# Transposes of 128x128 blocks on TensorE split into pairs of 64-row halves, with every engine's order rebuilt

## The reference, cut to what matters

```
scores = jnp.einsum('bach,baCh->bacC', k, q)
attn = jax.nn.softmax(masked / np.float32(np.sqrt(D_HEAD)), axis=-1)
z = jnp.einsum('bacC,baCh->bach', attn, v)
...
q = l2norm(q) * qs
k = l2norm(k) * ksc
q, k = rotary_xpos(q, k)
o = local_attention(q, k, v)
x = x + o @ wo
...
h = a * jax.nn.gelu(g, approximate=False)
x = x + h @ w2 + b2
```

## Time and profile before

| | |
|---|---|
| median of 3 runs | 1154.78 us (1153.16 to 1154.82) |
| the profiled execution's own time | 1154.38 us |
| its span, first to last instruction | 1152.6 us |
| PE busy | 1124.3 us, 98% of the span |
| PEld busy | 874.4 us, 76% |
| DVE, ACT, POOL busy | 790.9, 691.6 and 610.0 us |
| PE clock | granted 0.996 of full speed over the span |

### The profile page before, as it was taken

How to read it: one execution, slowest core, us unless ns; L and a number is a source line. 1 busy time by engine, 2 the same in 40 slices (tenths; PEclk the granted TensorE clock), 3 DMA queues, 4 the chain that set the end, 5 groups by cost and what they waited for, 6 DMA issues and landing times.

```text
span 1152.6 us, 20639 instructions
## 1 busy us (share of the span) xinstructions
PE 1124.3 (98%) x7114; PEld 874.4 (76%) x7114; DVE 790.9 (69%) x2417; ACT 691.6 (60%) x1712; POOL 610.0 (53%) x641
## 2 busy tenths in 40 slices
PE   8999999999999999999999999999999999999997
PEld 6777777777777766767667887877878878787676
DVE  6867677667767356778897677768667686675553
ACT  3668677777767224453676647657656566575832
POOL 1456666666664322049896446557465474573330
PEclk9999999999999999999999999999999999999999
DMA  7003333323210401030040001200002100001010
GB/s 255 1 2 132 100 109 113 123 93 123 89 71 2 164 19 55 1 112 22 19 176 1 2 1 36 94 1 1 1 19 99 55 1 1 1 32 42 19 38 18
DMA packets 30310, 64.72 MB, mean 56 GB/s; under 512 B 3840, under 2 KB 16256, under 8 KB 29696
## 3 DMA queue, kind: packets, MB, share of 16 engines
q1 hardware_dynamic: 30208, 63.41, 15.7%
HBM read 41.04 MB, written 22.36 MB: 55 GB/s over the span
## 4 chain that ended last, share of the span: by engine, by line
PE 90%; DVE 4%; POOL 2%; ACT 2%; issue 1%; DMA 0%; DVEq 0%; ACTq 0%; POOLq 0%
PE psum L1532 48%; PE psum L1633 7%; PE psum L1598 6%; PE psum L1615 6%; PE psum L1765 5%; PE psum L1814 5%; PE psum L1799 4%; PE psum L1781 4%; PE psum L1747 2%; PE psum L1827 1%; PE psum L1838 1%; PE psum L1721 1%; POOL rn L780 1%; PE psum L1829 0%; DVE y L1091 0%
## 5 line engine op out<-in xcount | busy, mean ns | idle before, releaser
L735 POOL TENSOR_TENSOR probs<-probs,rden 128x128 f32<-128x128 f32 (+3 forms) x256 | 177.6, 725 | 80.6 <-DVE rden L1149 80.6
L974 ACT ACTIVATE lp<-lp,lneg,rn 128x256 f32<-128x256 f32 (+1 forms) x256 | 143.6, 568 | 11.6 <-DVE lneg L1366 11.5
L890 ACT ACTIVATE probs<-probs,negmax 128x128 f32<-128x128 f32 (+3 forms) x256 | 139.9, 553 | 5.8 <-DVE negmax L1144 5.8
L1134 DVE CUSTOM_DVE_ANT_0 probs<-psum,causal 128x128 f32<-128x128 f32 (+3 forms) x256 | 110.3, 487 | 19.4 <-PE psum L1598 19.3
L768 POOL TENSOR_TENSOR lp<-lp,lrden 128x128 f32<-128x128 f32 x64 | 25.6, 400 | 165.8 <-DVE lrden L1371 165.8
L780 POOL TENSOR_TENSOR rn<-ssm,neg_half 128x8 f32<-128x8 f32 x64 | 108.4, 1693 | 0.0
L1354 DVE CUSTOM_DVE_ANT_0 lp<-psum,local 128x256 f32<-128x256 f32 (+1 forms) x256 | 84.2, 385 | 20.6 <-PE psum L1765 20.6
L771 POOL TENSOR_TENSOR lp<-lp,lrden 128x768 f32<-128x768 f32 x64 | 93.9, 1467 | 0.0
L1532 PE MATMUL psum<-wqkv_hi,hT_lo 128*128 128x512 f32 x192 | 82.0, 427 | 0.1
L961 ACT ACTIVATE sq<-psum 128x512 f32<-128x512 f32 x64 | 38.0, 594 | 68.9 <-PE psum L1532 68.9
L1633 PE MATMUL psum<-pT,v 128*64 128x256 f32 (+3 forms) x512 | 77.7, 446 | 1.4 <-DVE pT L1158 1.0
(11 more groups left out here) (172 smaller groups left out, 3146.7 us busy)
## 6 DMA issues: line engine op xcount, KB each, us to landing
w_raw<-in_w_all SPq DMA_DIRECT2D x22, 380.0 KB, 3.1
w_scratch<-w_half SPq DMA_DIRECT2D x22, 380.0 KB, 2.3
w_scratch<-w_rest SPq DMA_DIRECT2D x22, 380.0 KB, 3.0
x<-in_x SPq DMA_DIRECT2D x8, 512.0 KB, 7.4
aw<-in_w_quads SPq DMA_DIRECT2D x4, 768.0 KB, 5.5
wqkv_lo<-w_scratch SPq DMA_DIRECT2D x6, 512.0 KB, 6.3
wqkv_hi<-w_scratch SPq DMA_DIRECT2D x6, 512.0 KB, 4.5
w_hi<-w_scratch SPq DMA_DIRECT2D x2, 1364.0 KB, 6.5
```

Source lines behind the costliest of these rows:

```text
L735: ins = pool.tensor_tensor(pr, pr, rden[:, u % 2, h, i:i + 1].broadcast_to([P, TRI[i]]), ALU.mult)
L890: ins = act.activation(pr, pr, ACT.Exp, bias=negmax[:, u % 2, h, i:i + 1], scale=ADH ** -0.5, accum_out=den[:, u % 2, h, i:i + 1])
L974: ins = act.activation(pr, pr, ACT.Exp, bias=lneg[:, u % 2, h, w:w + 1], scale=rn[:, m % 2, w, 0, 2 * j + h:2 * j + h + 1], accum_out=lden ...
L1134: ins = dve.tensor_tensor_reduce(probs[:, u % 2, h, TRI_AT[i]:TRI_AT[i + 1]], bank[:, at:at + TRI[i]], causal[:, S - TRI[i]:S], 1.0, -3e38 ...
```

## The change

Each transpose of a 128x128 block becomes two: rows 0 to 63 of the block are transposed by the upper half of the array into 64 columns of one bank, rows 64 to 127 by the lower half into 64 columns of another. This is done for all probabilities (causal and local) and for the rotated q and k; transposes of `x`, `y` and the normalized inputs stay whole. The number of copies out of PSUM and their elements stay the same, but their destination has runs of 64 with gaps of 64. The banks, the groups (8, 8 and 4 blocks in a causal unit, two banks each) and all order strings are new.

```diff
-T_BANKS = (4, 5, 2, 3, 4, 5)
-Z_BANK = 4
+T_BANKS = ((4, 5), (2, 3), (4, 5))
...
-T_TILES = ((0,), (1, 3), (2,))
+T_BLOCKS = (((0, 0), (0, 1), (0, 3)), ((1, 0), (1, 1), (1, 3)), ((0, 2), (1, 2)))
...
-        UNIT_PE = ("sA@2 z sB@2 pv@2 pk@3 pq@3 t0@1 t1@1 t2@1 t3@1 t4@1 t5@1")
+        UNIT_PE = ("sB@2 z pk@3 pq@3 pv@3 t0@1 t1@1 sA@3 t2@1")
...
-        UNIT_ACT = ("e0@1 e1@1 pv@2 aw2@2 pk@3 aw0@3 pq@3 aw1@3 t1@1 t3@1 part@1 t5@1")
+        UNIT_ACT = ("e1@-1 pk@1 aw0@1 pq@1 e0 t1@-1 t3@-1 aw1@1 t5@-1 pv@1 part@-1 aw2@1")
...
             if what == "z":
-                take((what, *at), Z_BANK)
+                turn((what, *at), "p")
...
+                if u >= 2 and part == "sA":
+                    for n in (4, 5):
+                        wait_full(dve, plan["t", u - 2, n])
...
-                for c in T_TILES[k]:
-                    for i in range(c, T):
-                        lo = TRI_AT[i] + c * P
-                        ins = pe.transpose(bank[:, at:at + P], probs[:, u % 2, h, lo:lo + P], ident[:, :])
-                        at += P
-                ins.then_inc(full[use[0]], 1)
+            def transposes(u, g):
+
+                pe.wait_ge(s_prob, 2 * u + (1 if g == 0 else 2))
+                uses = [plan["t", u, 2 * g + half] for half in range(2)]
+                banks_of = [wait_free(pe, use) for use in uses]
+                blocks = [(h, i, c) for h, c in T_BLOCKS[g] for i in range(c, T)]
+                for n, (h, i, c) in enumerate(blocks):
+                    lo = TRI_AT[i] + c * P
+                    for half in range(2):
+                        rows = slice(half * HP, (half + 1) * HP)
+                        ins = pe.transpose(banks_of[half][:, n * HP:(n + 1) * HP], probs[rows, u % 2, h, lo:lo + P],
+                                           ident[rows, rows])
+                        if n == len(blocks) - 1:
+                            ins.then_inc(full[uses[half][0]], 1)
...
+                        for half in range(2):
+                            rows = slice(half * HP, (half + 1) * HP)
+                            ins = pe.transpose(banks_of[half][:, at:at + HP], ra[rows, t % 2, i, j * P:(j + 1) * P],
+                                               ident[rows, rows])
...
+                        for half in range(2):
+                            rows = slice(half * HP, (half + 1) * HP)
+                            ins = pe.transpose(banks_of[half][:, at:at + HP], lp[rows, u % 2, h, lo:lo + P],
+                                               ident[rows, rows])
```

More of the change, by code:

```diff
@@ L15 @@
 P = 128
+HP = P // 2
 B, S, D = 4, 512, 256
@@ L312, in unit_at @@
             return c, j, j // 2, 2 * c + j % 2
[L316 to L321, removed]
@@ L388, in build @@
-        CLOSE_POOL = ("sum.0 soft.30.1 soft.31.0 soft.31.1 last.6 norm.7 last.7 sum.1")
+        START_PE = ("xT.0 pq.0 pk.0 xT.1 pv.0 sA.0 sB.0 pk.1 pq.1 pv.1 sA.1 sB.1 pq.2 xT.2 pk.2 t.0.0 pv.2 "
+                    "t.0.1 t.0.2 sA.2 sB.2 z.0 pk.3 xT.3 pq.3")
+        START_DVE = ("xs.0 xn.0 aw.0.0 xs.1 xT.0 aw.0.1 xs.2 xn.1 pq.0 aw.0.2 pk.0 xT.1 xs.3 sA.0 sB.0 pk.1 "
+                     "pq.1 xn.2 sA.1 r.0.0 sB.1 r.0.1 xT.2 pq.2 xn.3 t.0.0 pk.2 t.0.2 t.0.4 sA.2 r.1.0 sB.2 "
+                     "r.1.1 z.0 pk.3 xT.3 pq.3")
@@ L389, in build @@
+        CLOSE_POOL = ("soft.30.1 soft.31.0 soft.31.1 sum.0 sum.1 last.6 norm.7 last.7")
         MLP = ("stats", "sh", "norm", "apply", "hnT", "hT")
@@ L484, in build @@
             if what == "t":
-                take((what, *at), T_BANKS[at[1]])
+                for half in range(2):
+                    take((what, at[0], 2 * at[1] + half), T_BANKS[at[1]][half])
             if what == "z":
-                take((what, *at), Z_BANK)
+                turn((what, *at), "p")
             if what == "awo":
@@ L524, in build, with transposed @@
                 take(("S", at[0], 1, what), 1)
+        def transposed(bank, n):
+            g, half = divmod(n, 2)
+            if g < 2:
+                dst = pT[:, g, 0:KEYB_AT[2]].rearrange("p (b s q) -> p b s q", s=2, q=HP)[:, :, half, :]
+                return bank[:, :].rearrange("p (b q) -> p b q", q=HP), dst
+            dst = pT[:, :, KEYB_AT[2]:TRI_AT[T]].rearrange("p h (b s q) -> p h b s q", s=2, q=HP)[:, :, :, half, :]
+            return bank[:, 0:2 * LOC // 2].rearrange("p (h b q) -> p h b q", h=2, q=HP), dst
         def wait_free(pe, use):
@@ L894, in evac_pT @@
             def evac_pT(u, n):
-                h, k = divmod(n, 3)
                 use = plan["t", u, n]
-                bank = wait_full(act, use)
-                at = KEYB_AT[T_TILES[k][0]]
-                w = sum(KEYB[j] for j in T_TILES[k])
-                copy(pT[:, h, at:at + w], bank[:, 0:w]).then_inc(read[use[0]], 1)
+                src, dst = transposed(wait_full(act, use), n)
+                copy(dst, src).then_inc(read[use[0]], 1)
             def evac_x1T(b):
@@ L981, in evac_T @@
                 bank = wait_full(act, use)
-                copy(lpT[:, h, 0:S], bank[:, :]).then_inc(read[use[0]], 1)
+                copy(lpT[:, h, :].rearrange("p (b s q) -> p b s q", s=2, q=HP)[:, :, 0, :],
+                     bank[:, 0:LOC_N // 2].rearrange("p (b q) -> p b q", q=HP)).then_inc(read[use[0]], 1)
             def evac_O(u):
@@ L1151, in evac_pT @@
             def evac_pT(u, n):
-                h, k = divmod(n, 3)
                 use = plan["t", u, n]
-                bank = wait_full(dve, use)
-                at = KEYB_AT[T_TILES[k][0]]
-                w = sum(KEYB[j] for j in T_TILES[k])
-                dve.tensor_copy(pT[:, h, at:at + w], bank[:, 0:w]).then_inc(read[use[0]], 1)
+                src, dst = transposed(wait_full(dve, use), n)
+                dve.tensor_copy(dst, src).then_inc(read[use[0]], 1)
             def evac_z(u):
@@ L1741, in transposed_qk @@
             def transposed_qk(m, t):
-                for i, (what, done) in enumerate((("Tq", l_q), ("Tk", l_k))):
+                uses = [plan[what, m, t] for what in ("Tq", "Tk")]
+                banks_of = [wait_free(pe, use) for use in uses]
+                for i, done in enumerate((l_q, l_k)):
                     pe.wait_ge(done, T * m + t + 1)
-                    use = plan[what, m, t]
-                    bank = wait_free(pe, use)
                     for j in range(FPAIRS):
-                        ins = pe.transpose(bank[:, j * P:(j + 1) * P], ra[:, t % 2, i, j * P:(j + 1) * P], ident[:, :])
-                    ins.then_inc(full[use[0]], 1)
+                        at = (i * FPAIRS + j) * HP
+                        for half in range(2):
+                            rows = slice(half * HP, (half + 1) * HP)
+                            ins = pe.transpose(banks_of[half][:, at:at + HP], ra[rows, t % 2, i, j * P:(j + 1) * P],
+                                               ident[rows, rows])
+                            if i and j == FPAIRS - 1:
+                                ins.then_inc(full[uses[half][0]], 1)
             def local_scores(u, part):
@@ L1773, in local_transposes @@
                 pe.wait_ge(l_prob, 2 * u + h + 1)
-                for k in range(2):
-                    use = plan["T", u, h, k]
-                    bank = wait_free(pe, use)
-                    at = 0
-                    for c in (2 * k, 2 * k + 1):
-                        for w in range(c, min(c + 2, T)):
-                            lo = loc_at(w) + (P if w == c and w else 0)
-                            ins = pe.transpose(bank[:, at:at + P], lp[:, u % 2, h, lo:lo + P], ident[:, :])
-                            at += P
-                    ins.then_inc(full[use[0]], 1)
+                uses = [plan["T", u, h, half] for half in range(2)]
+                banks_of = [wait_free(pe, use) for use in uses]
+                at = 0
+                for c in range(T):
+                    for w in range(c, min(c + 2, T)):
+                        lo = loc_at(w) + (P if w == c and w else 0)
+                        for half in range(2):
+                            rows = slice(half * HP, (half + 1) * HP)
+                            ins = pe.transpose(banks_of[half][:, at:at + HP], lp[rows, u % 2, h, lo:lo + P],
+                                               ident[rows, rows])
+                            if at == (LOC_N // P - 1) * HP:
+                                ins.then_inc(full[uses[half][0]], 1)
+                        at += HP
             def local_values(u):
```

85 lines of the change are left out of this document (40 added, 45 removed), and 70 rows, old and new, of tables (CLOSE_DVE, ENTRY_ACT, ENTRY_DVE, ENTRY_PE).

## The result

The changed kernel takes 1140.45 us (median of 4 runs, 1139.71 to 1140.73); the kernel before took 1153.97 beside it (4 runs, 1151.73 to 1154.82). The ratio is 0.9885, with an interval of 0.9868 to 0.9902. So the change makes it faster, by 13.5 us and not by the 41 that I forecast. The time lies inside my wide range (1088 to 1153), which was drawn around the rivals too, and outside the 1100 to 1122 that I gave to the forecast by itself.

The account below looks back on a forecast made before the run. PE's instruction list was taken to bound the kernel: 1154.4 - 63.9 (PE alone) + 17.4 (causal loop) + 4.7 (entry and close) + 1 (steps) = 1113.6 us, or 1113; range 1088 to 1153.

Parts of the forecast that it names:

- A pair for 0.06: All 1344 split transposes: a pair of 64-row transposes costs 0.06 us for a block's 0.109, 65.9 us less.
- middle: Rival: a pair costs 0.085 us because of the pace at which four instructions are issued; 1129 us, chance 0.14.
- no-gain: Rival: a pair costs as a block, 0.105 to 0.109 us, loads at the scores' pace; 1151 to 1157, chance 0.09.
- slower: Rival: halves go one after another or at the rows' issue pace, 0.12 us a pair; 1171 us, chance 0.15.
- Modes, 0.2 each: PE's changes of mode go from 282 to 292 at 0.2 us each, 2.0 us more.
- The loop in the causal units, 10.62: A loop through ACT's exponentials and copies, longer than PE's own work, sets the unit at 10.62 us; 17.4 us not had.
- falls inside the same 0.6: Causal units: z's copy and DVE's kl, whose bank pv waits for, add nothing beyond PE's 0.4 to 0.6 us wait.
- PE's own 10.05: Causal unit: PE's own work falls from 11.23 by 20 x 0.049 + 0.2 to 10.05 us.
- I estimate 1 us for all steps: Steps: needing both banks and both copies at once costs 1 us in all; a step saves 3.3 of 76 us.
- The close, forecast at 0: Close, about 50 pairs: PE is not alone on the path; no change in the stretch's time.
- The entry, forecast at -2.5: Entry of the local layers, 142 pairs: PE is not alone on the path; 2.5 us less.
- the loop does not bind: Rival: in the causal units ACT has less before it or PE arrives later; 17.4 us less, 1096 us, chance 0.15.

Follow-up runs that it names:

- experiment 3: Changed kernel with pk's product in bank 0, no longer in a bank shared with pv: 1135.22 us, 0.9841 of the kernel before.
- experiment 4: Changed kernel with the first head's exponentials ahead of the copy of k in ACT's causal-unit order: 1155.58 us, 1.0021 of the kernel before.
- experiment 5: Changed kernel with both pk's product in bank 0 and the first head's exponentials ahead of the copy of k: 1126.15 us, 0.9765 of the kernel before.
- Experiment 6: Changed kernel with the last k tile moved ahead of two MLP items in DVE's step order: 1141.36 us, 0.9896 of the kernel before.
- experiment 8: Kernel of experiment 1, but PE waits for each bank only where it is first written: 1176.12 us, 1.0191 of the kernel before.
- experiment 2: Pairs of 64-row transposes with all order strings, score banks and z's bank of the kernel before: 1149.76 us, 0.9969 of the kernel before.
- experiment 7: Changed kernel with the four close order strings of the kernel before: 1133.17 us, 0.9827 of the kernel before.
- experiment 1: Changed kernel with its new orders and banks, but each 128x128 block transposed whole again: 1181.16 us, 1.0240 of the kernel before.
- experiment 9: Changed kernel with pk's product in bank 0, the first head's exponentials ahead of k's copy, and the old close strings: 1122.73 us, 0.9730 of the kernel before.

## Why the prediction was right in direction and wrong in size

Against the profiled execution's own time my sum was 1113.6, and it came out at 1140.6: 27 us too little. By its own terms:

- **A pair for 0.06: right.** The rows show 0.062, and PE's busy time fell by 36 us, the two lines of transposes by 23 and 20. The middle, no-gain and slower rivals rested on the pace of issue and of loads; four instructions pass in 0.062 us, or 15.5 ns each. The 0.002 above my 0.06 is 3 us over all pairs. The Trainium skill ("TensorE: Matmul & The Clock Gate", section "Wait — 56ns, not 53.3ns?") has about 62 ns a matmul where the hardware decoder is off, which would have made a pair 0.124. The trace has half of that: no such floor holds in these runs, and none of them shows whether the decoder is on.
- **Modes, 0.2 each: right** where two kinds meet. From the large group to the scores I had nothing, and about 0.06 is left.
- **The loop in the causal units, 10.62: the mechanism right, a term too small.** `sB` takes 1.53 and not 1.43, the release to PE 0.14 that I had left out; with the others 10.81. And I wrote that `kl` and `pv`'s bank "falls inside the same 0.6". It does not fall inside: experiments 3 to 5 show a second one, as long as the first within 0.1, that had to be opened with it. PE's own 10.05 was too small as well: with both open the unit takes 10.40 (experiment 5), which the loop hid here. 28 units at 0.21 are 5.9 us. The rest of the causal stretch saved more than I gave it, so that this stretch is off by 2.
- **"I estimate 1 us for all steps": this step failed, and it is the largest miss.** A step saved 1.2 us and not 3.3: of the 4.1 us less for transposes and 1.0 more for modes, new waits took about 2, 13 us in all. `AV1` waits 0.9 of it; the rest, 0.1 to 0.4 each, is ahead of `Ta1`, `Tb1`, `AV2` and `AV3` on PE's timeline, and what those wait for no run took away. I had counted DVE busy for 299 of 400 us, where the earlier trace rows has 299 of 420, and had concluded that nothing would bind. But a share of idle time says nothing about what a new order has in front of each bank. Experiment 6 shows the bank at `AV1`, experiment 8 a price of two banks at once (0.8 a step, with whole blocks). The new order is no way around it: with all orders of before the six steps take 442.5 us, 1.0 less (experiment 2).
- **The close, forecast at 0: +6.7.** The order is 4.2 of it (experiment 7): score products that had filled the wait for ACT's copies now stand behind the transposes of unit 29, which wait for them. Without pairs the new order costs 4.7 there too (experiment 1), and with all orders of before the close takes 90.6 (experiment 2). The 2.5 that experiment 7 leaves open is not settled.
- **The entry, forecast at -2.5: +2.7.** About half of this miss goes with the clock. In the changed kernel 0.95 over 108.8 us is 10.9 us at the lower level; in experiments 3, 5 and 6 it is 0.98, some 4 us, and the same stretch takes 106.4 or 106.5, in 7 and 9 0.95 and 108.8 to 109.2. So 2.4 us of the 5.2 that I was off go with the step from 0.98 to 0.95; all 10.9 us, at 0.36 each as in this step, would be 4. The rest is in the order and its waits: at 0.98 whole blocks in the new order take 108.1 (experiment 1), 2.0 more than before, and pairs 106.4, so that the 142 pairs gain 1.7 there where I counted 3.5. No experiment filled PE's waits there to hold the clock up, so it is read from executions, and not tried. Why one execution falls and another does not stays open.
- **No term for the clock at all.** It is inside the last two points and not beside them. I took PE's list as the cost and gave waits their own length; in the close the products behind the waits of 3.10 and 1.82 us also ran at half pace.

The rivals: "the loop does not bind", 1096, is wrong, yet with both waits opened the unit comes to 10.40; the others fell with the pair's cost. My forecast's own range of 1100 to 1122 was for the loop's terms and the copies, and left out any wait in the steps beyond 1 us. That was the fault in it. The wide range held the result only because it had been drawn around rivals whose mechanisms did not happen; that is luck.

## What to carry to other kernels

A gain on the busiest engine is worth what the next loop leaves of it. So sum up every loop through a shared bank before you give the engine's saving to the kernel, the ones that are "nearly covered" above all: here two were within 0.1 us of each other, opening either alone gave -5 and +15 us, and both gave -14. When work that stood as cover for another engine gets shorter, the order has to be rebuilt with it: pairs alone gave 4 us, the order alone lost 27, together they gave 13.5. But rebuild it only where the cover was lost: in the steps and the close the order of before, with pairs in it, was as fast or faster. And a wait of PE can cost more than its length: look at the granted clock of the stretch behind each new long wait.

## What the runs showed of the hardware

- Float32 transposes of 64 rows on the two halves of the array run side by side: 16 pairs with their 32 loads in 1.02 us, 31 ns for a matmul with its load, where a whole block with its load takes 109.
- PE passed one instruction per 15.5 ns there, two loads and two matmuls in 0.062 us.
- About 0.06 us from 64-row transposes to scores that also use 64 rows (the first pair of scores needs 0.31 where the next needs 0.23), against 0.19 across a change of mode.
- Copies from PSUM whose destination has runs of 64 with gaps of 64 take no longer than those without: 0.685 us on DVE for 0.686, 0.58 on ACT for 0.60.
- In one kernel a mean clock lower by 0.001 goes with about 1 us more in 1150 (19 executions, from 1149.7 at 1.000 to 1155.4 at 0.994). That is also the whole spread of its times.
